# The causal mask of the score maxima: from TensorE matmuls to a masked reduction on VectorE, with another order of TensorE's work in a position

## The reference, cut to what matters

```python
att = jnp.einsum('bhqd,bhkd->bhqk', q, k) * SCALE
causal = jnp.tril(jnp.ones((T, T), dtype=bool))
att = jnp.where(causal, att, -jnp.inf)
att = jax.nn.softmax(att, axis=-1)
y = jnp.einsum('bhqk,bhkd->bhqd', att, v)
```

## Time and profile before

| | |
|---|---|
| median of 3 runs | 4954.11 us (4949.99 to 4957.22) |
| the profiled execution | 4944.35 us |
| its span, first to last instruction | 4942.5 us |
| TensorE busy over the span | 4181.8 us, 85% |
| VectorE, ScalarE, GpSimd busy | 52%, 38%, 20% |
| the attention stage | from the start to about 1420 us |
| one turn in its steady part | 170.44 us |

### The profile page before, as it was taken

How to read it: one execution, slowest core, us unless ns; L and a number is a source line. 1 busy time by engine, 2 the same in 40 slices (tenths; PEclk the granted TensorE clock), 3 DMA queues, 4 the chain that set the end, 5 groups by cost and what they waited for, 6 DMA issues and landing times. The chain is left out here.

```text
span 4942.5 us, 76401 instructions
## 1 busy us (share of the span) xinstructions
PE 4181.8 (85%) x28056; PEld 3105.4 (63%) x28056; DVE 2569.8 (52%) x5949; ACT 1874.8 (38%) x2968; POOL 970.5 (20%) x1013
## 2 busy tenths in 40 slices
PE   5999999999975999999999999999970399999930
PEld 2444444444434777777778877777750398989930
DVE  3676677677735444444455544444440254454546
ACT  1566566566643333333333333333310233233300
POOL 3233334243322000000000000000006300000056
PEclk8999999899978999999999999999985699999965
DMA  4343334234302000000000000000003222121146
GB/s 71 67 88 71 58 67 83 48 64 88 63 18 70 14 14 14 8 8 14 14 14 14 14 14 14 14 14 14 9 26 108 79 68 76 62 63 58 46 127 159
DMA packets 192067, 238.61 MB, mean 48 GB/s; under 512 B 28012, under 2 KB 169291, under 8 KB 191680
## 3 DMA queue, kind: packets, MB, share of 16 engines
q1 hardware_dynamic: 152896, 180.32, 15.9%
q0 software_dynamic: 12288, 26.83, 2.2%
q10 hardware_dynamic: 26496, 26.22, 1.6%
HBM read 102.41 MB, written 86.11 MB: 38 GB/s over the span
## 5 line engine op out<-in xcount | busy, mean ns | idle before, releaser
L781 ACT ACTIVATE probs<-a_scores 128x1024 f32<-128x1024 f32 (+3 forms) x768 | 614.9, 812 | 400.0 <-PE a_scores L685 394.6
L937 DVE TENSOR_REDUCE mx<-a_scores 128x2 f32<-128x1024 f32 (+3 forms) x512 | 518.4, 1021 | 209.8 <-PE a_scores L668 121.5
L1688 DVE TENSOR_TENSOR l_a<-l_general,l_a 128x512 f32<-128x512 f32 x64 | 44.3, 692 | 736.8 <-PE l_general L1318 736.8
L234 POOL TENSOR_TENSOR l_ln_rstd<-l_ln_ve,minus_half 128x4 f32<-128x4 f32 x80 | 82.9, 1036 | 1669.6 <-DVE l_ln_ve L207 1669.6
L685 PEld LDWEIGHTS a_scores<-q_st,k_st 50*128 50x128 f32 x1536 | 149.6, 192 | 395.1 <-issue 359.0
L685 PE MATMUL a_scores<-q_st,k_st 50*128 50x512 f32 (+3 forms) x1536 | 351.5, 455 | 28.9 <-issue 24.9
L705 PE MATMUL a_out<-probs,v_aug 128*32 128x512 f32 (+3 forms) x3072 | 345.4, 523 | 2.0 <-POOL probs L874 2.0
L668 PE MATMUL a_scores<-k_st,q_st 48*128 48x512 f32 (+3 forms) x1536 | 305.4, 395 | 44.4 <-ACT probs L781 31.1
L2126 PE MATMUL e_out<-e_weights_hi,e_hT_lo 128*128 128x256 f32 x1088 | 304.1, 279 | 0.0
L2126 PE MATMUL e_out<-e_weights_lo,e_hT_hi 128*128 128x256 f32 x1088 | 304.0, 279 | 0.0
L2126 PE MATMUL e_out<-e_weights_hi,e_hT_hi 128*128 128x256 f32 x1088 | 304.0, 279 | 0.0
(11 more groups left out here) (239 smaller groups left out, 9642.5 us busy)
## 6 DMA issues: line engine op xcount, KB each, us to landing
q_st<-parts SPq DMA_DIRECT2D x192, 128.0 KB, 4.6
k_st<-parts SPq DMA_DIRECT2D x192, 128.0 KB, 6.5
expert_rows_scratch<-zero SPq DMA_DIRECT2D x8, 2176.0 KB, 12.6
e_weights<-in_L_ffn_W_dram SPq DMA_DIRECT2D x16, 1024.0 KB, 6.3
e_rows<-expert_rows_scratch SPq DMA_DIRECT2D x24, 384.0 KB, 3.3
expert_out_scratch<-e_y ACTq DMA_DIRECT2D x24, 384.0 KB, 2.5
x_in<-in_L_attn_x_dram SPq DMA_DIRECT2D x8, 1024.0 KB, 5.4
x_res<-in_L_attn_x_dram SPq DMA_DIRECT2D x8, 1024.0 KB, 5.4
```

The source lines that it names most:

```text
L781: nc.scalar.activation(probs[:, k % 3, 2 * pair:2 * pair + 2, 0:w], psum_r[:, R.slot(u), :, 0:w], ACT.Exp).then_inc(R.evacuated[R.slot(u)], 1)
L937: nc.vector.tensor_reduce(out.rearrange("p h a -> p (h a)"), psum_r[:, R.slot(u), :, 0:w], AX.X, ALU.max).then_inc(R.evacuated[R.slot(u)], 1)
```

## The change

Three things change in the attention stage.

- `masked` and its operands go. The set-up loses the eight DMAs that placed them (L357) and the wait for these.
- A diagonal tile is now evacuated by two `tensor_tensor_reduce`, one for each head: each adds a float32 mask of the tile's width (the last 128 columns masked) to the scores, writes the sum back over the scores in PSUM, and gives the row's maximum. The slot is free behind the second. An unmasked tile keeps its TENSOR_REDUCE.
- PE's order in a position is S0, M0, S1, V, unit, M1, where it was S0, M0, V, S1, M1, unit. DVE does its `take` of the unit of position k in position k, ahead of the reduction of M1, where it was in position k + 1 ahead of M0.

```diff
-                def masked(u, h2, cols, mask):
...
                         last = nc.tensor.matmul(psum_r[:, R.slot(u), h2, 0:w],
                                                 q_st[rows, 2 * hg + pair, j * P:(j + 1) * P],
                                                 k_st[rows, 2 * hg + pair, k0:k1], start=True,
-                                                stop=(k1 != (j + 1) * P), skip_group_check=True)
-                    if k1 == (j + 1) * P:
-                        for h2 in range(2):
-                            last = masked(u, h2, slice(w - P, w), mqh)
+                                                stop=True)
                     last.then_inc(R.full[R.slot(u)], 1)
...
                         if more:
                             maxima(b + (k + LM) // NK, b, RU, k + LM, 0)
+                        scores(b, RU, k, 1)
                         if k > 1:
                             values(b, RU, k - 2)
                         elif with_tail:
                             values(b - 1, RU_TURN, NK - 2 + k)
-                        scores(b, RU, k, 1)
+                        if k in UNIT_AT and kept(UNIT_AT[k], with_head, with_tail):
+                            unit(batch_of(b, UNIT_AT[k]), b, U, UNIT_AT[k])
                         if more:
                             maxima(b + (k + LM) // NK, b, RU, k + LM, 1)
-                        if k in UNIT_AT and kept(UNIT_AT[k], with_head, with_tail):
-                            unit(batch_of(b, UNIT_AT[k]), b, U, UNIT_AT[k])
...
-                    nc.vector.tensor_reduce(out.rearrange("p h a -> p (h a)"),
-                                            psum_r[:, R.slot(u), :, 0:w],
-                                            AX.X, ALU.max).then_inc(R.evacuated[R.slot(u)], 1)
+                    if k1 == (j + 1) * P:
+
+                        dve.sem_inc(masking, 1)
+                        for h2 in range(2):
+                            s = psum_r[:, R.slot(u), h2, 0:w]
+                            last = nc.vector.tensor_tensor_reduce(
+                                s, s, mask[:, HALF - w:HALF], 1.0, LEAST, ALU.add, ALU.max, out[:, h2, :])
+                    else:
+                        last = nc.vector.tensor_reduce(out.rearrange("p h a -> p (h a)"),
+                                                       psum_r[:, R.slot(u), :, 0:w], AX.X, ALU.max)
+                    last.then_inc(R.evacuated[R.slot(u)], 1)
...
-                        what = UNIT_AT.get(k - 1)
-                        if what and what[0] in ON_DVE and kept(what, with_head, with_tail):
...
                         if with_tail and k - 1 in TAIL_SUM:
                             ln_t.sum_third(dve, b - 1, chain_t)
+                        what = UNIT_AT.get(k)
+                        if what and what[0] in ON_DVE and kept(what, with_head, with_tail):
...
                         if more:
                             reduce(b, b, RU, mk, 1)
```

More of the change, by code:

```diff
@@ L24 @@
 NEG = -1e30
+LEAST = -3.4e38
 H0, DH0 = 16, 16
@@ L251, in apply, with softmax_layer @@
                                             ALU.subtract, ALU.mult)
-def softmax_layer(nc, ident, ident_bf, minus_half, x_rows, W_qkv, b_qkv, W_proj, b_proj, weight,
+def softmax_layer(nc, ident, minus_half, x_rows, W_qkv, b_qkv, W_proj, b_proj, weight,
                   disha, x2_dram, rows_dram, y_dram):
@@ L293, in softmax_layer @@
         bias_p = sb("bias_p", [P, D])
-        mask_qk = sb("mask_qk", [P, P], BF16)
-        idh = sb("ident_halves", [P, 2, P], BF16)
-        mqh = sb("mask_qk_halves", [P, 2, P], BF16)
+        mask = sb("mask", [P, HALF])
         x_in = sb("x_in", [P, TT, D])
@@ L321, in softmax_layer @@
         made = sem("a_masks_made")
-        halves = sem("a_halves_placed")
         turned = sem("a_weight_turned")
@@ L351, in _ @@
                                          allow_slow_non_contiguous=True).then_inc(load, 16)
-                sp.wait_ge(made, 2)
-                for h2 in range(2):
[L354 to L358, removed]
                 sp.wait_ge(load, 16 * (8 + 8 * HB))
@@ L386, in _ @@
             def _(pool):
-                nc.gpsimd.memset(mask_qk[:, :], 0.0).then_inc(made, 1)
+                nc.gpsimd.memset(mask[:, :], 0.0).then_inc(made, 1)
                 pool.wait_ge(made, 1)
-                nc.gpsimd.affine_select(out=mask_qk[:, :], in_=mask_qk[:, :], compare_op=ALU.is_ge,
-                                        fill=NEG, base=0, pattern=[[-1, P]],
+                nc.gpsimd.affine_select(out=mask[:, HALF - P:HALF], in_=mask[:, HALF - P:HALF],
+                                        compare_op=ALU.is_ge, fill=NEG, base=0, pattern=[[-1, P]],
                                         channel_multiplier=1).then_inc(made, 1)
@@ L479, in softmax_layer @@
         rden_ready = sem("a_denominators_ready")
+        masking = sem("a_masking_begun")
         zeroed = sem("a_rows_zeroed")
@@ L1030, in turn @@
                         more = mk < NK or with_head
-                        what = UNIT_AT.get(k - 1)
-                        if what and what[0] in ON_DVE and kept(what, with_head, with_tail):
-                            of = (b - 1 if what[0] in TAIL_UNITS else
-                                  b + 1 if what[0] in HEAD_UNITS or what == ("N", 4) else b)
-                            take(of, b, U, what)
                         if more:
@@ L1053, in turn @@
                             ln_t.sum_third(dve, b - 1, chain_t)
+                        what = UNIT_AT.get(k)
+                        if what and what[0] in ON_DVE and kept(what, with_head, with_tail):
+                            of = (b - 1 if what[0] in TAIL_UNITS else
+                                  b + 1 if what[0] in HEAD_UNITS or what == ("N", 4) else b)
+                            take(of, b, U, what)
                         if more:
```

2 lines of the change are left out of this document (1 added, 1 removed).

## The result

| | before | changed |
|---|---|---|
| median | 4952.05 us (4945.61 to 4957.22, 4 runs) | 5329.8 us (5314.5 to 5342.01, 4 runs) |
| ratio | | **1.0763** [1.0743, 1.0784] |
| profiled execution | 4944.35 us | 5314.5 us |
| attention stage, first scores to last | 1310.9 us | 1666.9 us |
| of it at the lower clock | 133 us | 532 us |

The change makes the kernel 7.6% slower. The sign and the range (5070 to 5340) hold; the forecast of 5177 us is 153 us short. Of the 370 us between the two profiled executions the attention stage has 356; the rest of the program differs by 14.

The account below looks back on a forecast made before the run. PE's own work bounds the kernel; 37.2 + 6.5 + 1.6 - 8.3 - 6.3 - 2 = +28.7 us a turn, 7.67 turns +220, +6 and -2.5 elsewhere, together +223: 5168 profiled, 5177 us predicted, range 5070 to 5340.

Parts of the forecast that it names:

- The bound and the main term: Attention: PE sets the turn; in the new order S1 waits for the previous M1's reduction, +37.2 us a turn.
- A diagonal tile then takes 2 x (0.69 + 0.09) = 1.56: Masked reduction pair on DVE at 512 columns: 1.56 us, raising DVE's turn from 122 to 143 us.
- I take 0.44: Time from M1's start on PE to its reduction's start on DVE at 512 columns: 0.44 us.
- -8.3 us a turn: Gain from dropping the mask matmuls on PE, 0.13 us a tile over 64 diagonal tiles a turn.
- The take: DVE's moved take delays M1's reduction by 0.33 us in 20 positions, +6.5 us a turn; +1.6 for four N units.
- The old waits: M1's waits for the exponential of S0, 9.9 us a turn, go; two thirds taken, -6.3 us a turn.
- Set-up and first tiles: Set-up without mask placing -2.5 us; some 18 diagonal tiles ahead of the first turn +6 us.
- -2 us: Some 14 us near each turn's start at the lower clock, where the stall mostly vanishes: -2 us a turn.
- a rival with 0.10: Attention: low-clock stretch at each turn's start grows by 60 us, +20 us a turn, 5330 us; listed chance 0.10.
- a sign of being wrong: Attention: the prediction is wrong if the granted clock over a turn falls well below 0.96.
- The dearer sum over PSUM: Rival: DVE's write back to PSUM costs a second pass, 21 us a turn for M1, 5340 us; chance 0.12.
- The dear end of the prediction: Masked reduction pair on DVE at 512 columns with 0.25 us for each read: 1.88 us, kernel 5258.

Follow-up runs that it names:

- Experiment 4: Changed kernel with only V moved back ahead of S1 (S0, M0, V, S1, unit, M1): 5032.78 us, ratio 1.0157 to the kernel before.
- experiment 2: Kernel before, mask matmuls kept, with the changed order of TensorE and the moved take: 5156.44 us, ratio 1.0422 to the kernel before.
- experiment 7: Changed kernel without any masking in the maxima, every tile evacuated by one TENSOR_REDUCE: 5170.23 us, ratio 1.0475 to the kernel before.
- experiment 3: Changed kernel with VectorE's take back at its old place in the next position: 5312.94 us, ratio 1.0719 to the kernel before.
- experiment 5: Changed kernel with every M0 computed twice into its slot: 5237.6 us, ratio 1.0592 to the kernel before.
- experiment 6: Changed kernel with every M0 computed three times into its slot: 5206.21 us, ratio 1.0538 to the kernel before.
- Experiment 1: Changed kernel's masked reduction on VectorE, with TensorE's order and the take as before: 4947.19 us, ratio 0.9983 to the kernel before.
- experiment 8: Changed kernel with the unit behind M1 (S0, M0, S1, V, M1, unit) and the take at its old place: 5038.26 us, ratio 1.0184 to before.

## Why the prediction was right or wrong

**The bound and the main term: right.** S1 waits for the reduction of the last M1, V and the unit wait behind it. The release came 0.05 us after the reduction's end, as taken. Over the 43 positions that ran at the full clock in both kernels a turn rose from 147.7 to 177.5 us, +29.8; the forecast had +28.7 for all 48. Experiment 4 shows it as cause: V alone, put back, returned 298 us. That the two sums lie so close is luck, though: the mask matmuls were booked 7 us a turn too high as a gain and the takes nearly 7 us too high as a loss, as follows.

**Its parts: sizes off, which nearly cancel.**
- *"A diagonal tile then takes 2 x (0.69 + 0.09) = 1.56"*: the pair takes 1.39 us in position 31. The halves are 0.69 and 0.73 us, and the first read, 0.14 us, starts together with the second half and costs nothing. VectorE's turn is busy for 127 us, not 143.
- *"I take 0.44"* from M1's start to its reduction's start: 0.55, from 875.43 to 875.98. The reduction starts 0.04 us after M1's matmuls end before the change and 0.05 after it, but these take 0.50 us behind the unit, where they took 0.39 behind S1 (707.86 in the earlier trace rows). A pair behind V took 0.50 there too (707.52). The step was read off rows in which M1 stood in its old place.
- *"-8.3 us a turn"* for the mask matmuls: in the old order 40 positions gained 4.4 us in all; in the new order about 1 us (experiments 2 and 7). TensorE waits for VectorE there, and matmuls that leave it only lengthen the wait. This step was wrong in kind, and by 7 us a turn: a saving on an engine was booked in full on a path that by then ran through another one.

**The take: right at its place, wrong in sum.** It delays M1's reduction as said (experiment 3: 0.16 us in position 7, less than 0.33), but it also lets M0's reduction start sooner, and two of the four N positions lost 0.55 to 0.6 us without it, while the other two lost nothing. The +6.5 and +1.6 us a turn came to 1.3 us over 38 positions and to 18 us in the kernel at most, and the stage does not show even that. The +0.4 us for each N position was seen in no run; in two of the four the sign was reversed.

**The old waits: they went, as said.** M1's wait for the exponential went from 53.2 us in 920 us to 6.1 in the whole stage. What this gave by itself, -6.3 us a turn in the forecast, no run shows.

**Set-up and first tiles: small and right enough.** VectorE's first statistics start at 22.47 us instead of 24.76, -2.3. The first turn starts at 106.4 instead of 106.9 us, so the tiles ahead of it lost 1.8 where 6 was taken.

**The clock: the step that failed.** The forecast had *"-2 us"* a turn for it, as if the 14 us at each turn's start were all there is, and left the rest to a rival with 0.10. The stage had 532 us at the lower clock instead of 133, and the granted clock over a turn fell to 0.86, which the prediction named as a sign of being wrong. By the 0.27 above, the 399 us cost 107; the forecast on the profiled execution, 5168, would be 5275 with it (5292 by 0.31), against 5314.5. The rival itself (60 us more a turn, 20 us lost, 5330 us) came out nearly in full: 399 us over 7.67 turns are 52 a turn. It should have had the larger share. The rows that spoke against it were 13.6 us with pauses at 1.00; a short window before the stage was taken to speak for a thousand microseconds with a pause in each position. Experiments 5 and 6 show that what TensorE does in the pauses changes its clock: more matmuls in them, no step shorter, 80 and 112 us gained. The Trainium skill (TensorE: Matmul & The Clock Gate, A second HAM failure mode: psum-queue depth-cycling) says of a bf16 kernel that TensorE idling briefly between its groups of matmuls, as it cycles through PSUM banks, makes the clock go to and fro between its two levels. The trace agrees, here with float32 (1.00 and 0.50 both within single turns), and by that rule the rival was the one to weigh.

**The dearer sum over PSUM: refuted.** No second pass: a half of the new reduction over 512 columns takes 0.69 to 0.73 us, as the add of the earlier trace rows with 0.686. Experiment 1 has all of them and is no slower than before. The dear end of the prediction, 1.88 us for a pair, has 0.25 us for each read, which stands in no row; with the 0.17 of the earlier trace rows it would be 1.72. The pair took 1.39, with the second half starting 0.61 us after the first, before its 0.69 us were over. The Trainium skill (VectorE: DVE Perf Modes, Rules for kernel authors) says that each of a chain of instructions is drained whatever it is, so that their count should be kept low; at these instructions the trace does not bear out the draining.

**Left open.** What tells a stretch that keeps the full clock from one that loses it was not settled. In the changed kernel TensorE was busy for 54.22 us of 72 at 1.00 and for 37.06 us of 47.8 at 0.50 in other stretches, 75% and 78%:

```profile
600.00:672.00 72.00, 54.22 (x348) 25.18 (x350) 46.82 (x137) 39.21 (x55) 22.01 (x24) 1.00 0.38 60
938.90:986.70 47.80, 37.06 (x177) 16.90 (x170) 21.25 (x63) 18.27 (x27) 8.01 (x10) 0.50 0.40 79
```

The busy share does not separate them, and it is no fair measure either, since at 0.50 the same matmuls are busy for longer (values 1.86 us against 0.99, and the earlier trace rows).

## What to carry to other kernels

In a ring of slots, write down for each step which earlier tile's evacuation it waits for, and how much work of the same in-order engine stands between. With three slots, 1.0 us of matmuls cannot cover 0.55 + 1.22 + 0.05 us; one more piece of work behind the last tile (values or the unit, experiments 4 and 8) returned 290 to 298 us, and the order of work was worth far more than the 2048 matmuls saved. When an order opens a pause in every step, price the clock too: here about a third of the stage's loss, by the estimates above, was TensorE running slower. A saving on an engine that waits is to be booked at nothing; here it even cost clock.

## What was not expected of the hardware

- Giving TensorE more to do made the kernel faster: 5329.8, 5237.6 and 5206.21 us with M0 once, twice and three times, with the time at the lower clock at 532, 345 and 234 us.
- The reverse too: taking the mask matmuls off TensorE, with nothing else in its order moved, raised the time at the lower clock from 133 to 189 us in the profiled executions (experiment 1), which ate part of what they saved. In the new order it went from 170 to 258 us (experiments 2 and 7).
- A masked reduction in place over PSUM costs as much as a plain add of the same size, 0.69 to 0.73 us at 512 columns, and the read of its maximum, 0.14 us long, overlaps with the next instruction. Two of these take 1.39 us where one reduction of both heads takes 1.23.
